# Two heads' exponentials as one ScalarE instruction over two neighbouring PSUM banks

## What is computed

```
x = x + attn(layernorm(x))                   # self attention with rotary positions, full
x = x + xattn(layernorm(x), ctx)             # causal self attention + attention over ctx, one output projection
x = x + experts(layernorm(x))                # 16 experts, top 1, capacity 256
# each attention, for every batch and head:
p = softmax(q @ k.T * HEAD_DIM ** -0.5)      # 512 x 512, masked in the causal one
y = p @ v
```

## Time and profile before

| | us |
|---|---|
| median of 3 runs | 1539.83 |
| lowest and highest run | 1537.02, 1545.12 |
| the profiled execution | 1542.09 |
| its span, first to last instruction | 1540.3 |
| TensorE busy | 1408.5 (91%) |
| VectorE busy | 1195.1 (78%) |
| ScalarE busy | 1057.6 (69%) |
| mean granted TensorE clock | 0.978 |

### The profile page before, as it was taken

How to read it: one execution, slowest core, us unless ns; L and a number is a source line. 1 busy time by engine, 2 the same in 40 slices (tenths; PEclk the granted TensorE clock), 3 DMA queues, 4 the chain that set the end, 5 groups by cost and what they waited for, 6 DMA issues and landing times.

```text
span 1540.3 us, 37645 instructions
## 1 busy us (share of the span) xinstructions
PE 1408.5 (91%) x14527; PEld 632.2 (41%) x14527; DVE 1195.1 (78%) x2439; ACT 1057.6 (69%) x2139; POOL 655.2 (43%) x535
## 2 busy tenths in 40 slices
PE   3699999999999999999999999999999988689997
PEld 1222323322333433434334344343343432379896
DVE  6788888888877687787877877878778686557784
ACT  2378887788778677687777776776777767346562
POOL 3544664565523322434336234352453221336563
PEclk9699999999999999999999999999999999799999
DMA  5535434434324333333323242333233311077771
GB/s 178 130 94 161 139 110 113 135 103 121 100 57 112 78 114 94 108 112 98 83 84 108 81 117 75 101 98 82 90 104 92 88 37 45 29 259 246 279 241 54
DMA packets 119062, 175.25 MB, mean 114 GB/s; under 512 B 26113, under 2 KB 85735, under 8 KB 114280
## 3 DMA queue, kind: packets, MB, share of 16 engines
q1 hardware_dynamic: 110960, 157.94, 35.3%
q0 software_dynamic: 5888, 14.24, 2.8%
q10 hardware_dynamic: 2048, 0.83, 0.2%
HBM read 101.81 MB, written 51.15 MB: 99 GB/s over the span
## 4 chain that ended last, share of the span: by engine, by line
PE 63%; DVE 19%; ACT 8%; issue 5%; DMA 3%; POOL 1%; SPq 1%; POOLq 0%; DVEq 0%; ACTq 0%
PE psO L761 15%; PE psM L472 12%; DVE negmax L1240 11%; PE psS L784 11%; PE psK L815 7%; PE psK L472 7%; ACT probs L1049 6%; PE psS L472 4%; PE psK L706 2%; DVE xn L1188 1%; DVE mrows L1353 1%; DVE stats L1162 1%; PE psM L900 1%; DMA stack<-mrows 1%; PE psM L851 1%
## 5 line engine op out<-in xcount | busy, mean ns | idle before, releaser
L1240 DVE TENSOR_REDUCE negmax<-psS 128x1 f32<-128x512 f32 (+3 forms) x1536 | 867.5, 615 | 200.5 <-PE psS L784 112.0
L1049 ACT ACTIVATE probs<-psK 128x512 f32<-128x512 f32 (+3 forms) x1536 | 755.4, 546 | 288.4 <-PE psK L815 166.7
L761 PE MATMUL psO<-probs,V 128*32 128x256 f32 (+1 forms) x5632 | 439.5, 384 | 7.4 <-ACT U L1041 5.8
L784 PE MATMUL psS<-stack 48*128 48x512 f16 (+3 forms) x1536 | 282.2, 364 | 47.6 <-DVE negmax L1240 41.9
L815 PE MATMUL psK<-stack 50*128 50x512 f16 (+3 forms) x1536 | 275.2, 355 | 11.0 <-DMA stack<-mrows 5.2
L784 PEld LDWEIGHTS psS<-stack 48*128 48x128 f16 x1536 | 74.0, 93 | 359.7 <-DVE negmax L1240 300.2
L761 PEld LDWEIGHTS psO<-probs,V 128*32 128x32 f32 x5632 | 112.1, 108 | 187.8 <-issue 116.7
L1473 POOL TENSOR_TENSOR rstd<-lnt,minus_half 128x4 f32<-128x4 f32 x24 | 24.8, 1031 | 248.1 <-DVE lnt L1180 248.1
L815 PEld LDWEIGHTS psK<-stack 50*128 50x128 f16 x1536 | 75.4, 94 | 41.9 <-ACT probs L1049 19.7
L1610 POOL DMA_INDIRECT out_dram<-stack,put_to x32 | 76.7, 2398 | 17.9 <-issue 9.1
L472 PE MATMUL psM<-xT,wx 128*128 128x512 f16 x288 | 75.5, 382 | 1.6 <-DVE mrows L1353 0.6
(11 more groups left out here) (198 smaller groups left out, 2027.4 us busy)
## 6 DMA issues: line engine op xcount, KB each, us to landing
spare<-in_L_ffn_w_dram SPq DMA_DIRECT2D x32, 1024.0 KB, 6.3
parts_scratch<-parts SPq DMA_DIRECT2D x192, 128.0 KB
stack<-parts_scratch SPq DMA_DIRECT2D x96, 256.0 KB, 3.8
stack<-parts_scratch SPq DMA_DIRECT2D x96, 128.0 KB, 3.5
packed<-U SPq DMA_DIRECT2D x192, 64.0 KB
recipB<-recip_scratch SPq DMA_DIRECT2D x46, 256.0 KB
shared<-shared SPq DMA_DIRECT2D x48, 128.0 KB, 2.1
probs<-back_scratch POOLq DMA_DIRECT2D x16, 258.0 KB, 3.1
```

The costliest lines, as they stand in the source:

```text
L761: mm = nc.tensor.matmul(psO[32 * i:32 * i + 32, q0:q1], v_of(par)[:, kt, 2 * g + i % 2 + PAIRS * (i // 2), :], probs[:, (unit + i % 2) % P ...
L784: mm = nc.tensor.matmul(psS[:, banks[hh], 0:n], stack_of(par, 0)[rows, hp, qt * P:(qt + 1) * P], stack_of(par, 1)[rows, hp, 0:n], start=Tr ...
L1049: nc.scalar.activation(probs[:, t % P_RING, i, q0:T], psK[:, S_BANKS[t][i], q0:T], ACT.Exp, scale=SM_SCALE / (1 if b.kind == "A" else WSCA ...
L1240: nc.vector.tensor_reduce(negmax[:, g % 2, at:at + 1], psS[:, S_BANKS[u // 2][j], 0:n], AX_X, ALU.max, negate=True).then_inc(s["max_done"], 1)
```

## The change

In slots whose second bank is the first plus one, ScalarE waits until both heads' scores are there and takes both exponentials in one instruction, over the two banks as one operand, and raises `exp_done` by 2. These are the slots with banks (1, 2) and (0, 1): 21 of a stretch's 32. The slots with (2, 0) and (1, 0) keep one instruction for each head. TensorE's and VectorE's programs, the semaphores and all waits for them are as before.

```
                         if t % 2 == 0:
                             need(act, s["av_done"], b.at("av_done", b.av_count(t)))
-                        for i in range(2):
+                        scale = SM_SCALE / (1 if b.kind == "A" else WSCALE ** 2)
+                        at, nb = S_BANKS[t]
+                        if nb == at + 1:
+                            act.wait_ge(s["scores_k"], b.at("scores_k", 2 * t + 2))
+                            nc.scalar.activation(probs[:, t % P_RING, :, q0:T], psK[:, at:at + 2, q0:T], ACT.Exp, scale=scale
+                                                 ).then_inc(s["exp_done"], 2)
+                        for i in range(0 if nb == at + 1 else 2):
                             act.wait_ge(s["scores_k"], b.at("scores_k", 2 * t + i + 1))
                             nc.scalar.activation(probs[:, t % P_RING, i, q0:T], psK[:, S_BANKS[t][i], q0:T], ACT.Exp,
                                                  scale=SM_SCALE / (1 if b.kind == "A" else WSCALE ** 2)
                                                  ).then_inc(s["exp_done"], 1)
```

## The result

| | before | after |
|---|---|---|
| median, us (4 runs each) | 1539.92 | 1616.97 |
| lowest and highest run | 1537.02, 1545.12 | 1613.99, 1621.65 |
| profiled execution; its span | 1542.09; 1540.3 | 1616.63; 1614.8 |
| ScalarE busy | 1057.6 | 1032.8 |

The change makes the kernel slower: 1.0489 times the time before, 95% interval 1.0469 to 1.0509. That is 77 us where +58 was forecast, 1617 against 1598, inside the range. One run of experiment 2's first kernel, the profiled one, took 1722.82 us at a granted clock of 0.744 and is left out of its ratio, so that kernel's trace is not read here.

The account below looks back on a forecast made before the run. TensorE, 91% busy, was taken to bound the kernel, with ScalarE at 69%. Stalls of 83 us, less 22 given back and 3 gained, made +58 us: 1598 us forecast, range 1558 to 1635.

Parts of the forecast that it names:

- Rival 2: ScalarE paces the stretches, so the 504 savings count: 1515 us, or 1528 with half on the path; chance 0.05.
- rival 3: Stalls and savings alike do nothing that can be measured: 1532 to 1548 us; chance 0.04.
- Rival 1: TensorE's lead over ScalarE swallows the stalls, short slots borrowing from long: +30 us or less, 1555 to 1570; chance 0.10.
- signs named ahead: 504 fewer exponential rows, longer short slots and stretches, psK waits from under 25 us to 70 or more, psS waits down 10 to 25.
- A: Eight of the 24 attention stretches: stalls forecast at 29.3 us in all, 0.65 back in each, length near 57 us.
- B: Eight causal attention stretches with some narrower exponentials: stalls forecast at 23.8 us, 0.65 back in each, length near 51 us.
- C: Eight attention stretches where VectorE also routes: stalls forecast at 30.0 us, 1.4 back in each, length near 54 to 55.
- Part 3: Stalls given back in gaps where TensorE would have waited anyway, mostly for VectorE: 22 us back.
- Part 1: Work removed from ScalarE: joined exponential 1.04 us instead of 1.09 a pair, 25 us of busy time, 3 us gained.
- Part 2: TensorE's wait before the next score matmuls lasts until both heads' exponentials end: 83 us of stalls over some 274 slots.
- 0.03 for the later start: Joined instruction starts 0.03 us later (0 to 0.06), since it must wait for both heads' scores.
- rival 4: More than the sum: joined instruction without overlap, +44 us, or TensorE's clock falling more often, 0.9 each: 1635 to 1660; chance 0.08.

Follow-up runs that it names:

- experiment 2's first kernel: The changed kernel, but joined only in the 207 of 504 slots where TensorE has a job besides the maxima's transpose: 1543.02 us, 1.0004 times before.
- experiment 2: The changed kernel joined only in the 207 slots with a job (1543.02 us, 1.0004 times before), or only in the 297 without (1615.88 us, 1.0477).
- experiment 4: Kernel before, exponentials single, but count raised once, at the end of the second, in all 32 slots of a stretch: 1636.88 us, 1.061 times before.
- experiment 5: Changed kernel with joined slots raising the count by 1: 1610.14 us (1.0443 times before); again, 1605.73 beside the changed kernel rerun at 1619.81.
- Experiment 1: Kernel before, exponentials single, but in the 21 slots of neighbouring banks the count is raised once, at the second's end: 1616.42 us, 1.0484 times before.

## Why the prediction was right, and where it was off

**The bound and the direction** held. TensorE paced the kernel and ScalarE had time to spare, so saving 24.8 us of ScalarE (25 forecast) bought nothing that can be told (experiment 2), and a later release cost. Rival 2 is out with that, and rival 3 too. Rival 1, a lead that swallows the stalls, is out with the 77 us, and experiment 4 found no such limit either. Of the signs named ahead, the waits of psK, the slots and the stretches came (A 57.6 us, B 51.8, C with 55.3 a little over); the waits of psS for VectorE fell by 8 us where 10 to 25 were forecast, which belongs to Part 3.

**Part 1**, the joined instruction, was right: 1.027 us against 1.04, at the lower of its bounds (1.03 to 1.09), nearer to the continuation of the narrower exponentials, 1.03, than to the copy out of SBUF. The trace agrees here with the Trainium skill (ScalarE: Activation LUTs, What ACT_TABLE_LOAD costs), whose two figures make 1.04 as an estimate; its overlap of 93 ns is 0.11 in the rows, two times 599 less 1.09, and there the rows decide. The 3 us that this was to give on the chain can't be seen: 207 joined slots came out at 1.0004.

**Part 2**, the stalls, had the mechanism and the places. In A slots 0, 9, 12, 13, 16, 24, 27 and 28 were forecast to pay 0.48, 0.37, 0.36, 0.23, 0.43, 0.43, 0.37 and 0.36 us; they paid 0.48, 0.42, 0.37, 0.28, 0.44, 0.44, 0.42 and 0.38. The 0.03 for the later start was the mis-sized term: it is 0.095 in odd slots (0.414 to 0.510) and 0.057 in even ones (0.474 to 0.532), outside the bound of 0.06 in the odd ones. Part of it, up to 0.06, is the wait as an instruction of its own that comes with the step of 2; experiment 5 took it away and got back some 14 us. What is left with a step of 1, about 0.04, is near the forecast. Summed anew over the trace of before with the measured starts and 1.026 us the stalls are some 88 us, not 83: A 31.0, B 25.1, C 32.0. That is an estimate; it moves between 86 and 92 with how late starts in the trace of before are taken.

**Part 3**, what is given back, was sized too high, above all in B. In A 31.0 - 26.5 = 4.5 us came back (5.2 forecast), in C 32.0 - 20.1 = 11.9 (11.2). Gaps that were forecast for A did give back: in the stretch of the earlier trace rows slot 14 got shorter by 0.23 us behind slot 13, which paid 0.28, and slot 21 by 0.21 behind slot 19, which paid 0.21.

In B, where 5.2 were forecast, the stretches grew by 3.5 us more than the sum. That excess is the clock's (below). Five of the eight B stretches had no fall of it after and grew by 3.3 us each; in the one from 745.6 us on every slot grew by what its own stall makes, and no more than 0.12 us came back, in slot 10. The prediction does not list the gaps that it counted in B; a plain candidate is the 0.49 us that TensorE waits for VectorE ahead of slot 7's psS, behind the stalls of slots 3 and 4. That wait before, and after:

```profile
714.90 0.25 ACT L1090 ACTIVATE mrows<-psM 16x128 f16<-16x128 f32 x1
...
716.63 0.39 PE L784 MATMUL psS<-stack 48*128 48x512 f16 x2 [0.49 <-DVE negmax L1240]
```

```profile
754.71 0.25 ACT L1096 ACTIVATE mrows<-psM 16x128 f16<-16x128 f32 x1
...
754.99 0.28 DVE L1359 SCALAR_TENSOR_TENSOR mrows<-psM,mrows 16x128 f16<-16x128 f32 x1 [0.58 <-ACT mrows L1096]
755.20 0.72 DVE L1194 TENSOR_SCALAR xn<-X,lnt,rstd 128x256 f32<-128x256 f32 x2
...
756.44 0.39 PE L784 MATMUL psS<-stack 48*128 48x512 f16 x2 [0.49 <-DVE negmax L1246]
```

It is still 0.49 us, and from the evacuation's start to these scores it is 1.73 us in both. VectorE is late there because it waits for the maxima's rows, which ScalarE evacuates (L1096) behind slot 5's exponentials, and these were late by the stalls of slots 3 and 4. So the gap moved along with what I thought would run into it. The row that I had missed is VectorE's wait for that evacuation, over the kernel before and after:

```profile
DVE mrows L1353 <- ACT mrows L1090: 24.9, 65, 1.9
```

```profile
DVE mrows L1359 <- ACT mrows L1096: 47.1, 72, 2.4
```

**The clock**, in rival 4, did come in. One B stretch after, with a granted clock of 0.97, took 53.3 us, others alike 51.8 at 1.00:

```profile
636.80:690.10 53.30, 48.98 (x613) 22.24 (x614) 38.84 (x88) 31.17 (x61) 20.71 (x17) 0.97 0.36 94
```

Before, no B stretch had a fall, and it was the first A and late C stretches that had one (for C see the earlier trace rows). In the attention part I count seven falls of 3.4 or 6.8 us after, five before. Two of the B stretches with a fall had none in the changed kernel's second trace (experiment 5) and were 1.5 to 1.6 us shorter there, more than the 0.9 that rival 4 took for a fall. Three of the eight B stretches had one after, some 4.6 us as an estimate from these two; without that B grew by 24 us, near the sum of 25.1, and about 1 of the 5.2 came back. Against that the first A stretch had a fall before and none after; it grew by 2.0 us, the five behind it by 3.2 to 3.5, so part of A's 4.5 is the clock's too. In all the clock is a few us of the 77 and not its cause.

Together: stalls of 88 us in place of 83, nothing gained in place of 3, and 13 us given back in place of 22, with the clock's few us counted in. That makes 75, as the attention part grew, where the forecast had 58.

The Trainium skill's rule that the prediction set beside the sum (Perfetto Trace Analysis, Optimizing Scalar/DVE Operations) agrees with the trace: grouping on an engine that was not saturated (69%) won nothing, and the bubbles came on another, TensorE (129.4 us of waits, 19.7 before). Experiment 1 adds that no grouping is needed for these bubbles; a count raised late is enough.

## What to carry to other kernels

Before two instructions are joined, look at who waits for the end of the first: the count that it raised is a release, and joining puts that release off by the second half's time, with no wait edited anywhere. The price is found slot by slot, as the loop of release and refill against the time from one issue to the next in the trace, and not from the mean slot. A gap gives a stall back only if its own releaser does not hang on the work that is late; follow that chain one engine further than the row shows. And before a remainder of a few us is put down to gaps, compare the granted clock of the stretches.

## What was not expected of the hardware

- An instruction that raises a count by 2 had its wait as an instruction of its own ahead of it; with a step of 1 the wait is within it. The difference is about 0.06 us in odd slots (0.510 against 0.453 us after the scores), 0.02 in even ones, which have a second wait anyway, and some 14 us over the kernel (experiment 5).
- TensorE's granted clock can fall in the middle of dense work. Just behind two stalls, of 0.36 and 0.53 us, of the B stretch that took 53.3 us it went to a mean of 0.56, most of that window at the lower of its two levels, 1.2 GHz, and an AV of eight matmuls took 1.08 us instead of 0.64. A window ahead of the fall and one in it:

```profile
671.60:678.10 6.50, 5.05 (x56) 1.84 (x52) 5.75 (x11) 3.58 (x7) 4.63 (x4) 1.00 0.47 135
678.20:681.60 3.40, 3.40 (x26) 1.36 (x28) 0.83 (x3) 1.23 (x3) 0.00 (x0) 0.56 0.79 246
```

Ahead of it TensorE was busy 5.05 of 6.50 us with two waits for exponentials; other B stretches with the same waits kept the full clock, so what decides was not found.
